# A rank-32 product inside a tuned two-layer linear kernel: from split operands on the whole TensorE array to plain float32 on four column tiles

## The reference, cut to what matters

```python
# W, W1: 1024 x 1024; A[b]: 1024 x 16, Bm[b]: 16 x 1024 (picked by itok_B_0_23)
y = x + (x @ W.T + b0 + 2 * (x @ A[b]) @ Bm[b])
# A1[b]: 16 x 1024, B1[b]: 1024 x 16 (picked by itok_B_6_15)
out = y + (y @ W1.T + b1 + (y @ A1[b].T) @ B1[b].T)
```

## Time and profile before

| | |
|---|---|
| median of 3 runs | 292.08 us |
| profiled execution | 292.03 us |
| span of its trace (first to last instruction) | 290.2 us |
| PE busy | 285.5 us (98%) |
| DVE busy | 216.5 us (75%) |
| ACT busy | 107.2 us (37%) |
| one batch (from 2 on) on PE | 22.0 us |

### The profile page before, as it was taken

One profiled execution on the slowest core, in us unless ns is written; L12 is line 12 of the kernel. 1 busy time (PEld: TensorE's weight loads), 2 busy tenths in 40 slices (PEclk: granted clock), 3 DMA queues, 4 the chain that ended last, 5 costly groups with the idle time before them and its releaser, 6 DMA issues.

```text
span 290.2 us, 3863 instructions
## 1 busy us (share of the span) xinstructions
PE 285.5 (98%) x1317; PEld 236.2 (81%) x1317; DVE 216.5 (75%) x331; ACT 107.2 (37%) x150; POOL 18.6 (6%) x43
## 2 busy tenths in 40 slices
PE   7999999999999999999999999999999999999996
PEld 5878888877878888878888888888888888888885
DVE  5789999999799999887874874874874774774313
ACT  4675364433688635332222232232132132132000
POOL 3333101400000001000000000000000000000000
PEclk9999999999999999999999999999999999999999
DMA  7997000100545450004504504504504513512002
GB/s 214 391 413 277 27 1 11 55 9 0 163 161 211 156 158 18 0 36 153 168 36 160 159 36 161 159 36 139 182 37 144 164 38 138 170 38 108 0 36 108
DMA packets 15367, 33.92 MB, mean 117 GB/s; under 512 B 2389, under 2 KB 2645, under 8 KB 15350
## 3 DMA queue, kind: packets, MB, share of 16 engines
q1 hardware_dynamic: 14178, 31.60, 31.5%
q0 software_dynamic: 1024, 2.10, 2.3%
q10 hardware_dynamic: 148, 0.00, 0.0%
HBM read 22.09 MB, written 11.60 MB: 116 GB/s over the span
## 4 chain that ended last, share of the span: by engine, by line
PE 98%; DVE 0%; issue 0%
PE bank L1189 17%; PE bank L1188 17%; PE bank L1190 17%; PE bank L1036 9%; PE bank L1040 9%; PE bank L1041 9%; PE bank L1214 5%; PE bank L1195 3%; PE bank L1075 1%; PE bank L1068 1%; PE bank L1070 1%; PE bank L1069 1%; PE bank L1056 1%; PE bank L1054 1%; PE bank L1055 1%; PE bank L1133 1%
## 5 line engine op out<-in xcount | busy, mean ns | idle before, releaser
L1188 PE MATMUL bank<-ops,late 128*128 128x512 f32 x192 | 75.0, 391 | 0.0
L1189 PE MATMUL bank<-ops,late 128*128 128x512 f32 x192 | 74.9, 390 | 0.0
L1190 PE MATMUL bank<-ops,late 128*128 128x512 f32 x192 | 74.8, 390 | 0.0
L461 ACT CAST late<-raw_a 128x512 fp32r<-128x512 f32 x48 | 29.4, 621 | 63.2 <-PE bank L1195 29.7
L1041 PE MATMUL bank<-ops 128*128 128x512 f32 x112 | 43.7, 390 | 0.0
L1040 PE MATMUL bank<-ops 128*128 128x512 f32 x112 | 43.7, 390 | 0.0
L1190 PEld LDWEIGHTS bank<-ops,late 128*128 128x128 f32 x192 | 36.1, 188 | 7.7
L1188 PEld LDWEIGHTS bank<-ops,late 128*128 128x128 f32 x192 | 36.1, 188 | 7.3
L1189 PEld LDWEIGHTS bank<-ops,late 128*128 128x128 f32 x192 | 36.1, 188 | 7.3
L1036 PE MATMUL bank<-ops 128*128 128x512 f32 x112 | 40.8, 403 | 0.2
L721 DVE TENSOR_TENSOR late<-raw_a,late 128x512 fp32r<-128x512 f32 x48 | 31.9, 687 | 0.2
(11 more groups left out here) (149 smaller groups left out, 374.9 us busy)
## 6 DMA issues: line engine op xcount, KB each, us to landing
raw_a<-xT SPq DMA_DIRECT2D x32, 256.0 KB, 4.3
out<-raw_a SPq DMA_DIRECT2D x27, 256.0 KB, 2.0
a<-rb_rows SPq DMA_DIRECT2D x8, 392.0 KB
raw_a<-W1T SPq DMA_DIRECT2D x2, 1024.0 KB, 12.8
raw_b<-W SPq DMA_DIRECT2D x2, 1024.0 KB, 16.4
rb_rows<-late SPq DMA_DIRECT2D x3, 512.0 KB
rb_rows<-b0w SPq DMA_DIRECT2D x3, 512.0 KB
raw_a<-U SPq DMA_DIRECT2D x4, 256.0 KB, 4.3
```

What stands on the lines that cost most here:

```text
L461: nc.scalar.copy(x_op(j, 0), x_raw(j)).then_inc(op_hi[j], 1)
L1188: mm(bank[:, :], hi, t_op(t, 0, k), start=(start and k == 0), stop=False, skip_group_check=not start)
L1189: mm(bank[:, :], hi, t_op(t, 1, k), start=False, stop=False, skip_group_check=not start)
L1190: last = mm(bank[:, :], lo, t_op(t, 0, k), start=False, stop=(k == KH - 1), skip_group_check=not start)
```

## The change

The factor product is computed in another form and at another place.

- It takes float32 operands and not split ones. x is read as it landed (`xr`), so the matmuls of batch b + 1 wait for x_landed and not for the splits. A float32 matmul with 256 columns stands once in the program; each of the 8 slices k has one matmul with 32 columns of weights, whose output is 32 partitions of the bank: slice k goes to partitions 32 (k mod 4) and on, which is column tile k mod 4 of the array (tile_size 128 x 32 in the built program). 8 matmuls a batch in place of 16.
- In batch 0 the raw quadrants have been overwritten by sums by then, so it takes x's high and low parts, read as float32: 16 matmuls.
- `h_product(b + 1)` stands in batch b, after p7 (in batch 0: after fill_z).
- `stack_h` adds four row groups of the bank in place of two: two more VectorE instructions per batch.
- `factors` copies the two factors (no splits). The memsets of the padding are gone.
- A21 is split in batch 0 alone: 7 casts on ScalarE and 7 subtractions on VectorE are gone. S3 and S4 get a place of their own from batch 1 on (`stage_q` 9 and 10), and the loads of x(b) from batch 2 on wait for h_summed.

```diff
-                for k in range(KT):
-                    kh, tok = k // KH, slice(k % KH * P, (k % KH + 1) * P)
-                    for part in range(2):
-                        last = mm(banks[6 + s][:, 0:T], aa[:, s, k * 4 * RK:k * 4 * RK + P],
-                                  x_first[part][:, 2 * kh:2 * kh + 2, tok],
-                                  start=(k == 0 and part == 0), stop=(k == KT - 1 and part == 1))
+                parts = [words(part) for part in x_first] if b == 0 else [xr]
+                for n, part in enumerate(parts):
+                    for k in range(KT):
+                        kh, tok, j = k // KH, slice(k % KH * P, (k % KH + 1) * P), k % TILES
+                        last = mm(banks[6 + s][j * CT:(j + 1) * CT, 0:T], aa[:, s, k, :],
+                                  part[:, 2 * kh:2 * kh + 2, tok], start=(k < TILES and n == 0),
+                                  stop=(k >= KT - TILES and n == len(parts) - 1))
                 last.then_inc(h_summed, 1)
...
             fill_z(0)
+            h_product(1)
             p3(0)
             for b in range(1, B):
                 p1(b)
-                h_product(b)
                 p6(b)
                 p2(b)
                 p5(b)
                 p7(b)
+                if b + 1 < B:
+                    h_product(b + 1)
                 p4(b)
...
-                nc.vector.tensor_copy(h_tmp, bank[2 * RK:4 * RK, 0:T]).then_inc(h_moved, 1)
-                dve.wait_ge(h_moved, b + 1)
+                nc.vector.tensor_copy(h_tmp, bank[CT:2 * CT, 0:T]).then_inc(h_moved, 1)
+                for j in range(2, TILES):
+                    dve.wait_ge(h_moved, b * (TILES - 1) + j - 1)
+                    nc.vector.tensor_tensor(h_tmp, bank[j * CT:(j + 1) * CT, 0:T], h_tmp, ALU.add).then_inc(h_moved, 1)
+                dve.wait_ge(h_moved, (b + 1) * (TILES - 1))
...
-                nc.vector.tensor_copy(to[:, :, 0:RK], a0).then_inc(aa_hi, 1)
-                nc.vector.tensor_copy(to[:, :, RK:2 * RK], g).then_inc(aa_hi, 1)
-                dve.wait_ge(aa_hi, b * 2 + 2)
-                nc.vector.tensor_tensor(to[:, :, 3 * RK:4 * RK], g, to[:, :, RK:2 * RK], ALU.subtract)
-                nc.vector.tensor_tensor(to[:, :, 2 * RK:3 * RK], a0, to[:, :, 0:RK], ALU.subtract).then_inc(aa_ready, 1)
+                nc.vector.tensor_copy(aa[:, s, :, 0:RK], a0_raw[:, s, :].rearrange("p (k r) -> p k r", k=KT)
+                                      ).then_inc(aa_ready, 1)
+                nc.vector.tensor_copy(aa[:, s, :, RK:2 * RK], g_all[:, :, b * RK:(b + 1) * RK]).then_inc(aa_ready, 1)
...
+                    if b >= 2:
+                        sp.wait_ge(h_summed, b)
                     sp.dma_start(xr[:, j, :], xT[b, :, j, :]).then_inc(x_landed[j], DMA)
...
                     high_x(A11, b + 1)
-                    high_x(A21, b + 1)
                     high_x(S2, b + 1)
```

More of the change, by code:

```diff
@@ L41, in lora_pair @@
     B, _, _, QW = xT.shape
+    TILES = 4
+    CT = P // TILES
     assert U11.shape[0] == W0.shape[1] * GROUP == KH
@@ L50, in lora_pair @@
     BR = B * RK
-    assert BR == P and NH == 2 and QW == KH * P == HALF
+    assert BR == P and 2 * RK == CT and NH == 2 and QW == KH * P == HALF
     STACK = 6 * RK + 2
-    AA_W = KT * 4 * RK + 4 * RK
     ORDER_M7 = (1, 2, 3, 0)
@@ L145, in x_op @@
             return late[:, part if j <= A22 else 2 + part, (j % 4) * HALF:(j % 4 + 1) * HALF]
-        s_raw = {S1: rows[:, 0, :], S2: rows[:, 1, :], S3: xr[:, A21, :], S4: xr[:, A12, :]}
-        def x_raw(j):
-            return xr[:, j, :] if j <= A22 else s_raw[j]
         stage_q = raw_a[:, 0:3, :].rearrange("p s (k n) -> p (s k) n", n=HALF)
@@ L160, in lora_pair, with s_raw, x_raw @@
         c21, c22, c12 = u2, u3, u4
+        def s_raw(j, b):
+            if b == 0 and j in (S3, S4):
+                return xr[:, A21 if j == S3 else A12, :]
+            return {S1: rows[:, 0, :], S2: rows[:, 1, :], S3: stage_q[:, 9, :], S4: stage_q[:, 10, :]}[j]
+        def x_raw(j, b):
+            return xr[:, j, :] if j <= A22 else s_raw(j, b)
         banks = [ctx.enter_context(nc.psum_tensor(f"bank{i}", [P, HALF], F32)) for i in range(8)]
@@ L263, in load_x @@
                     if b >= 1:
-                        sp.wait_ge(op_lo[j], b)
+                        if j != A21 or b == 1:
+                            sp.wait_ge(op_lo[j], b)
                         for s in {A11: (S2, S3), A21: (S1, S3), A12: (S4,), A22: (S1,)}[j]:
                             sp.wait_ge(s_made[s], b)
-                        if j in (A21, A12):
+                        if j in (A21, A12) and b == 1:
                             sp.wait_ge(op_lo[S3 if j == A21 else S4], b)
+                    if b >= 2:
+                        sp.wait_ge(h_summed, b)
                     sp.dma_start(xr[:, j, :], xT[b, :, j, :]).then_inc(x_landed[j], DMA)
@@ L453, in high_x @@
                 if b >= 1:
-                    if j == A21:
+                    act.wait_ge(p_done[LAST_USE[j]], b)
+                    if j <= A22 and b == 1:
                         act.wait_ge(h_summed, b)
[L457 to L461, removed]
+                nc.scalar.copy(x_op(j, 0), x_raw(j, b)).then_inc(op_hi[j], 1)
             def keep_p1(b):
@@ L592, in _ @@
             high("t4")
-            for j in (A11, A21):
-                high_x(j, 1)
+            high_x(A11, 1)
             put_c11(0)
@@ L727, in sum_s1 @@
                     dve.wait_ge(op_lo[S1], b)
-                nc.vector.tensor_tensor(s_raw[S1], xr[:, A21, :], xr[:, A22, :], ALU.add).then_inc(s_made[S1], 1)
+                nc.vector.tensor_tensor(s_raw(S1, b), xr[:, A21, :], xr[:, A22, :], ALU.add).then_inc(s_made[S1], 1)
             def sum_s2(b):
@@ L734, in sum_s2 @@
                 dve.wait_ge(s_made[S1], b + 1)
-                nc.vector.tensor_tensor(s_raw[S2], s_raw[S1], xr[:, A11, :], ALU.subtract).then_inc(s_made[S2], 1)
+                nc.vector.tensor_tensor(s_raw(S2, b), s_raw(S1, b), xr[:, A11, :], ALU.subtract).then_inc(s_made[S2], 1)
             def sum_s3(b):
-                dve.wait_ge(op_lo[A21], b + 1)
-                nc.vector.tensor_tensor(s_raw[S3], xr[:, A11, :], xr[:, A21, :], ALU.subtract).then_inc(s_made[S3], 1)
-            def sum_s4(b):
-                dve.wait_ge(op_lo[A12], b + 1)
+                if b == 0:
+                    dve.wait_ge(op_lo[A21], 1)
+                else:
+                    dve.wait_ge(x_landed[A11], (b + 1) * DMA)
+                    dve.wait_ge(x_landed[A21], (b + 1) * DMA)
+                    if b == 1:
+                        dve.wait_ge(lo[SLOT["t1"]], filled("t1", 1))
+                    dve.wait_ge(op_lo[S3], b)
@@ L744, in sum_s4 @@
+                nc.vector.tensor_tensor(s_raw(S3, b), xr[:, A11, :], xr[:, A21, :], ALU.subtract).then_inc(s_made[S3], 1)
+            def sum_s4(b):
+                if b == 0:
+                    dve.wait_ge(op_lo[A12], 1)
+                else:
+                    dve.wait_ge(x_landed[A12], (b + 1) * DMA)
+                    if b == 1:
+                        dve.wait_ge(lo[SLOT["t1"]], filled("t1", 1))
+                    dve.wait_ge(op_lo[S4], b)
                 dve.wait_ge(s_made[S2], b + 1)
-                nc.vector.tensor_tensor(s_raw[S4], xr[:, A12, :], s_raw[S2], ALU.subtract).then_inc(s_made[S4], 1)
+                nc.vector.tensor_tensor(s_raw(S4, b), xr[:, A12, :], s_raw(S2, b), ALU.subtract).then_inc(s_made[S4], 1)
@@ L765, in stack_h @@
                 dve.wait_ge(h_summed, b + 1)
-                nc.vector.tensor_copy(h_tmp, bank[2 * RK:4 * RK, 0:T]).then_inc(h_moved, 1)
-                dve.wait_ge(h_moved, b + 1)
+                if b >= 1:
+                    dve.wait_ge(h_added, b)
+                nc.vector.tensor_copy(h_tmp, bank[CT:2 * CT, 0:T]).then_inc(h_moved, 1)
[3 more added lines that the diff above has]
+                dve.wait_ge(h_moved, (b + 1) * (TILES - 1))
                 if b == 0:
                     dve.wait_ge(t_landed, DMA)
-                nc.vector.scalar_tensor_tensor(out=h_sum[:, :], in0=bank[0:2 * RK, 0:T], scalar=t_cols[:, b:b + 1],
+                nc.vector.scalar_tensor_tensor(out=h_sum[:, :], in0=bank[0:CT, 0:T], scalar=t_cols[:, b:b + 1],
                                                in1=h_tmp, op0=ALU.add, op1=ALU.add).then_inc(h_added, 1)
@@ L964, in _ @@
                 nc.vector.memset(h_stack[s][6 * RK:6 * RK + 2, :].bitcast(F32), 1.0).then_inc(ones_set, 1)
[L965 to L968, removed]
             dve.wait_ge(lo[SLOT["t3"]], filled("t3", 1))
@@ L981, in _ @@
             make_u3(0)
-            for j in (A11, A21, A12):
+            for j in (A11, A12):
                 low_x(j, 1)
@@ L1003, in _ @@
                     low_x(A11, b + 1)
-                    low_x(A21, b + 1)
                 make_u2(b)
@@ L1295, in p7 @@
                 product(b, S3, T3, Y, False).then_inc(p_done[7], 1)
-            pe.wait_ge(pad_set, 2)
             p1(0)
```

20 lines of the change are left out of this document (10 added, 10 removed).

## The result

The changed kernel takes 287.29 us (median of 4 runs, 287.15 to 288.08) against 292.26 us (292.01 to 292.88) for the kernel before: a ratio of 0.984, interval 0.982 to 0.986. It is faster by 5.0 us; 288.8 was forecast. The profiled execution took 287.28 us with a span of 285.7 us, 4.5 us shorter than the span before. A second set of runs beside the experiments gave 287.11 us against 292.26, ratio 0.982 (0.979 to 0.985).

A forecast was written before the change was run, and what follows sets the result against it. PE was taken as the bound, 98% busy and without waits. Batches 1 to 7 gave -3.6 us and batch 0 +0.35, together -3.2, side effects nothing: 292.03 - 3.2 = 288.8 us, range 285.0 to 299.5.

The forecast's parts named there:

- PE bounds, and nobody becomes late: Whole kernel: PE runs without a wait from 2 us to the last matmul, and no other engine becomes late.
- the cover named for x's loads, for p1's copy and for VectorE's chain: Side effects costed at nothing: 3.7 us of cover for x's loads, 2.1 for p1's copy; DVE's chain to u2 gets shorter.
- The choice between the two ends: Factor product in batches 1 to 7: 3.44 us without tile overlap or 0.86 with four side by side; 0.86 was taken.
- the first case: Factor product: four tiles side by side, change of shape at any price between its bounds; chance 0.50, range 284.7 to 290.3.
- Four tiles side by side, 0.86 us: Factor product: four column tiles always overlap, 0.86 us a batch, 1.72 in batch 0, against 1.89 before.
- The 3.17x: Factor product: speedup for four column tiles, by proportion from 2.38x for three; 1.09 us a batch, about -1 us in all.
- The end of no overlap: Rival for the factor product: tiles do not overlap, 3.44 us a batch, 6.88 in batch 0; +20 us, 312 us; chance 0.06.
- The change of shape, 0.52 us: Around each factor product, switching to 32-column tiles and back: 0.33 us for two emptyings plus 0.19 for one bare weight load.
- The sum: All factor products: -3.6 us in batches 1 to 7, +0.35 in batch 0, together -3.2 us, giving 288.8 us.
- fill_z(0): Batch 0's wait for u4, 0.15 us before: DVE later by 0.2 us, PE by 0.35 or more, so costed at 0.
- The blocking pair: Rival in the factor product: a float32 matmul's second instruction blocks PE's queue, 1.94 us a batch; +6.3 us, 298.3; chance 0.34.
- The gain is eaten: Rival: tiles overlap with losses, 1.6 to 1.75 us a batch in all, within 0.6 us of before; chance 0.08.

## Why the prediction was right, point by point

- *PE bounds, and nobody becomes late*: right from batch 1 on. No wait of PE there, so the cover named for x's loads, for p1's copy and for VectorE's chain held; and the place is worth nothing (287.58 against 287.29).
- *The choice between the two ends*: partly luck. No row of the kernel before could decide between 0.86 and 3.44 us, and the choice of 0.86 had a chance of 0.50. The range of 285.0 to 299.5 also took in a kernel that is 7 us slower, so that 287.29 lies in it says little; the first case's own range, 284.7 to 290.3, says more.
- *Four tiles side by side, 0.86 us*: right. Four start within 60 ns, a step is 0.216 to 0.22 us, and with one tile the same product takes 3.57 us. The 3.17x that the prediction took by proportion from the Trainium skill ("TensorE: Matmul & The Clock Gate", Part 3) is less than the rows show: 3.57 against 1.00 is 3.6x. The end of no overlap, which was forecast at +20 us, came out at +18.1 (310.08 against 291.97), smaller mostly by the change of shape.
- *The change of shape, 0.52 us*: this term was mis-sized. The extra visit costs 0.34 us at its place and 0.27 to 0.28 net. That is about the 0.33 for two emptyings alone; no room is left for the bare weight load of 0.19 that I had added. The rule of the Trainium skill that the prediction cites ("TensorEngine Tiling (Array Packing)", Key Properties), a drain at a change of the tiling mode, agrees in kind: the extra cost comes with each visit. That the array runs quite empty no row shows: the first L1233 starts at 212.53 and the row of the last L1203 lasts until 212.60, and on the way out it is 213.53 and 213.60. An overlap of 0.07 us is left of the usual 0.163, though the ends of rows are modelled.
- *The sum*: a batch was to cost 1.38 us for its product and costs 21.32 - (21.97 - 1.89) = 1.24. Seven batches are 7 x (-0.65) = -4.5 us in place of -3.6. Batch 0 has 1.86 and 0.43 - 0.23 = 0.20 for the first matmul after it, 2.06 - 1.89 = +0.17 in place of +0.35. Together -4.4, and with the longer wait at fill_z(0) below -4.3. The span shows -4.5: the last 0.2 lies ahead of batch 0's product, which stands at 116.61 and stood at 116.83. In the kernels that are unaltered up to there it stands between 116.2 and 117.2, so this part is scatter, and so may be the rest up to the 5.0 of the medians.
- *Of the 1.24 us*, 0.86 is the four steps and 0.34 the visit at its place. The last 0.04 us was not tested by itself.
- *The blocking pair*, at 0.34 the strongest rival: wrong here. The two instructions of a float32 matmul do not block the next tile. But the mechanism is in the chip one step further out: with four float32 matmuls in a row on a tile the queue stands, and batch 0 pays 2.7 us. I had put the limit at the second instruction; it is at the third matmul. The Trainium skill's rule of strict program order, which this rival leaned on ("TensorE: Matmul & The Clock Gate", Part 3, The mechanism), is not borne out for the starts. In the changed kernel the four that start within 60 ns are the first instructions of four pairs, and the second of the first pair starts later than all of them. Even with four in a row strict order would make 29 steps of 0.216, 6.3 us, where 4.53 was measured.
- *The gain is eaten*: its bounds were worked out a little low. With the prediction's own terms 1.6 us a batch gives -1.2 us in all, and only 1.67 to 1.80 us stays within 0.6. It did not come to that.
- *fill_z(0)*: costed at nothing, "VectorE later by 0.2, PE by 0.35 or more". This step failed, at a small price. u4, the two rank matmuls and the product behind them in the changed kernel:

```profile
129.33 0.68 DVE L819 TENSOR_TENSOR raw_a<-bank,raw_a 128x512 f32<-128x512 f32 x1
129.67 0.90 PE L1208 MATMUL bank<-a,b0w 98*128 98x512 f32 x2
130.50 1.07 PE L1233 MATMUL bank<-raw_a,aa 128*32 128x256 f32 x16
```

  From 129.67 to 130.50 it is 0.83 us, where the kernel with u4 earlier has 0.56. So 0.27 us are a wait for u4, in place of 0.15 before. Counted from batch 0's product, u4 came 0.31 us later than before (129.33 - 116.61 against 129.24 - 116.83) and PE only 0.18 (129.67 - 116.61 against 129.71 - 116.83). There was no room at all: 0.6 us more on VectorE (the split of A21) and 0.86 us less on PE (batch 0 in the cheap form) both turn almost whole into waits there.

## What to carry to other kernels

Where PE is the bound, try a product with 32 output rows on column tiles: here four side by side made float32 cheaper than split operands on the full width (1.24 against 1.89 us a batch). Give neighbouring float32 matmuls different tiles, or at most two in a row the same, and do the whole product in one visit, since each further visit costs a batch 0.27 us. Before taking work off the bounding engine at one place, look for the next hand-over behind it: if that engine waits there already, however shortly, and the other engine's chain starts ahead of what you shorten, the gain comes back as a wait.

## What the runs showed of the hardware that was not expected

- A column tile has a running float32 matmul and one waiting, or in instructions one and three; what comes behind them for the same tile stops the queue. With four in a row 0.9 us lie between the starts of neighbouring tiles (one run); with one or two in a row all four tiles start within 60 ns.
- Matmuls on different column tiles do not start in the program's order: the second instruction of a pair starts 0.22 us after its first, when the first ones of the next three tiles have started.
- A visit to the narrow tiles and back costs 0.34 us at its place, and 0.27 us by the period of the batch.
- A float32 matmul of 256 columns costs 0.216 us per instruction, two instructions each, in a 32-column tile as on the full width by proportion (0.43 for 512 columns in the earlier trace rows); reading four float32 streams at once costs nothing extra (3.57 us for 16 steps on one tile, 1.00 for 4 steps on four, which is 0.21 us a step for the 12 steps between).
